# The next batch's x rounded during heads 0 and 1 and split by GpSimd in two halves, and head 0's maxima taken with 128 rows

## The reference

```python
c_adj = mean(x, channels)                              # (1024,)
Wg = adj * (symmetric function of c_adj[n] - c_adj[m]) # (1024, 1024)
g = relu(x.T @ Wg * para)                              # (256, 1024), the queries q of 4 heads of 64
k, v = split(x @ kv_w)
out[h] = softmax(q[h] @ k[h].T * scale) @ v[h]         # for 4 heads
x1 = layernorm(x + out)
```

## Time and profile before

| | us |
|---|---|
| median of 3 runs | 2891.92 |
| the profiled execution's own time | 2890.31 |
| its span, first to last instruction | 2888.4 |
| TensorE matmuls busy | 2737.2 (95%) |
| VectorE busy | 1980.6 (69%) |
| ScalarE busy | 1658.9 (57%) |
| GpSimd busy | 1276.3 (44%) |

### The profile page before, as it was taken

How to read it: one execution, slowest core, us unless ns; L and a number is a source line. 1 busy time by engine, 2 the same in 40 slices (tenths; PEclk the granted TensorE clock), 3 DMA queues, 4 the chain that set the end, 5 groups by cost and what they waited for, 6 DMA issues and landing times. The chain is left out here.

```text
span 2888.4 us, 39341 instructions
## 1 busy us (share of the span) xinstructions
PE 2737.2 (95%) x12436; PEld 1844.3 (64%) x12436; DVE 1980.6 (69%) x2843; ACT 1658.9 (57%) x2146; POOL 1276.3 (44%) x684
## 2 busy tenths in 40 slices
PE   7999999999999999999999999997699999989964
PEld 5565665656656565665656656564588888878853
DVE  6787786877868687786877868684533333348878
ACT  6566576766667666576766667663422222237768
POOL 3755657565475755657565475745200000000015
PEclk9999999999999999999999999999899999999976
DMA  4123222232222223222232222221333222305556
GB/s 139 59 83 104 76 73 75 70 105 85 68 76 80 73 83 103 76 73 74 71 104 85 69 76 80 73 66 29 119 107 104 87 87 102 109 14 197 186 228 257
DMA packets 128224, 276.23 MB, mean 96 GB/s; under 512 B 12208, under 2 KB 62384, under 8 KB 124592
## 3 DMA queue, kind: packets, MB, share of 16 engines
q1 hardware_dynamic: 128176, 275.62, 29.8%
HBM read 178.79 MB, written 62.98 MB: 84 GB/s over the span
## 5 line engine op out<-in xcount | busy, mean ns | idle before, releaser
L304 POOL TENSOR_TENSOR psum<-psum,probs 128x1024 f32<-128x1024 f32 x320 | 783.7, 2449 | 147.1 <-ACT probs L372 123.1
L372 ACT ACTIVATE probs<-sc_ps 128x1024 f32<-128x1024 f32 x512 | 507.2, 1023 | 420.4 <-PE sc_ps L813 360.0
L544 DVE TENSOR_REDUCE mx<-mx_ps 128x1 f32<-128x512 f32 x768 | 519.6, 689 | 282.3 <-PE mx_ps L782 280.5
L829 PE MATMUL pv_ps<-probs,v 128*64 128x512 f32 x2048 | 492.4, 604 | 0.0
L813 PE MATMUL sc_ps<-qa,ka 128*128 128x512 f32 x1024 | 386.9, 403 | 0.0
L813 PE MATMUL sc_ps<-qb,kb 128*128 128x512 f32 x1024 | 379.5, 393 | 0.0
L782 PE MATMUL mx_ps<-ka,qa 128*128 128x512 f32 x768 | 315.2, 424 | 11.6 <-ACT v L358 4.7
L829 PEld LDWEIGHTS pv_ps<-probs,v 128*64 128x64 f32 x2048 | 125.6, 136 | 224.8 <-issue 194.4
L782 PEld LDWEIGHTS mx_ps<-ka,qa 128*128 128x128 f32 x768 | 138.5, 187 | 184.6 <-issue 88.9
L813 PEld LDWEIGHTS sc_ps<-qa,ka 128*128 128x128 f32 x1024 | 187.6, 188 | 105.0 <-issue 64.1
L1168 DVE TENSOR_TENSOR agg_lo<-ag_ps,agg_hi 128x1024 fp32r<-128x1024 f32 x32 | 39.2, 1224 | 312.1 <-ACT agg_hi L1095 312.1
(11 more groups left out here) (194 smaller groups left out, 5551.7 us busy)
## 6 DMA issues: line engine op xcount, KB each, us to landing
adj_ring<-in_adj_dram SPq DMA_DIRECT2D x128, 512.0 KB, 3.7
pre_scratch<-pre SPq DMA_DIRECT2D x28, 1024.0 KB, 4.5
pre<-pre_scratch SPq DMA_DIRECT2D x28, 1024.0 KB, 4.9
x<-in_x_dram SPq DMA_DIRECT2D x16, 1024.0 KB, 5.6
kb<-ka SPq DMA_DIRECT2D x64, 256.0 KB, 3.3
qa<-qa SPq DMA_DIRECT2D x64, 256.0 KB, 3.1
res<-in_x_dram SPq DMA_DIRECT2D x16, 1024.0 KB, 5.7
x_scratch<-res SPq DMA_DIRECT2D x16, 1024.0 KB, 4.5
```

The lines of the kernel that those rows point to most:

```text
L304: pool.tensor_tensor(psum[:, h % 2, :], probs[:, 0, :] if k == 1 else psum[:, h % 2, :], probs[:, k % PR, :], ALU.add).then_inc(s["pool_ad ...
L372: nc.scalar.activation(probs[:, i % PR, :], sc_ps[:, t % 2, :], ACT.Exp, scale=SCALE)\
L544: nc.vector.tensor_reduce(mx2[:, nh, n:n + 1], mx_ps[:, nh, :], AX.X, ALU.max)\
L829: ins = nc.tensor.matmul(pv_ps[nh * HD:(nh + 1) * HD, h % 2, :], v[:, i, h * HD:(h + 1) * HD], probs[:, i % PR, nh * BANK:(nh + 1) * BANK] ...
```

## The change

It has four parts.

- **Head 0's maxima with 128 rows.** A new instruction on VectorE, `double_q`, writes relu of head 0's product into the other 64 rows of `qa[0]`, right from `scr`, between the two `q_times_para`. It replaces `copy_qa(b, 0)`. `max_scores` uses all 128 rows in head 0 as in the others. It now waits for `q_doubled`; ScalarE's first `relu_q`, which overwrites `scr`, waits for it too.
- **x rounded later.** The 8 tiles of `x_high` leave the stretch around `v_copy` and stand two by two behind the pairs 2 and 3 of head 0 and 0 and 1 of head 1.
- **x split in halves.** `split_x` is two instructions of 128x1024 on GpSimd, one before the additions of head 1 and one before those of head 2, each behind the last addition of the head before. TensorE's and SyncE's waits for `x_split` count two per batch.
- **Order.** In head 0 the scores' part 1 of tile 0 now stands before the first maxima of head 1 (`MAX_HALVES[0]`), and SyncE sends the row of head 0 before `copy_kb` of head 1.

```diff
-    MAX_HALVES = [[[2, 1, 1], [1, 1, 1, 1, 0], [2, 1, 1, 1, 1], [1, 1, 0, 0, 0]]] + \
+    MAX_HALVES = [[[0, 2, 1], [2, 1, 1, 1, 0], [2, 1, 1, 1, 1], [1, 1, 0, 0, 0]]] + \
...
-                copy_qa(b, 0)
                 copy_qa(b, 1)
+                store_row(b, 0)
                 copy_kb(b, 1)
-                store_row(b, 0)
...
+            def split_x(b, half):
+                tiles = slice(T // 2 * half, T // 2 * (half + 1))
+                wait(pool, s["x_split"], 2 * b + half)
+                wait(pool, s["pool_added"], POOL_ADDS * (4 * (b - 1) + half + 1))
+                wait(pool, s["xhi_done"], T * b + T // 2 * (half + 1))
+                pool.tensor_tensor(x_lo[:, tiles, :], x32[:, tiles, :], x_hi[:, tiles, :].bitcast(F32), ALU.subtract)\
                     .then_inc(s["x_split"], 1)
...
-                if not last:
-                    split_x(b + 1)
-                    wait(pool, s["x_split"], b + 2)
                 wait(pool, s["ql_done"], 4 * b + 4)
                 for h in range(HEADS):
+                    if not last and h in (1, 2):
+                        split_x(b + 1, h - 1)
+                        wait(pool, s["x_split"], 2 * b + 2 + h)
...
             def relu_q(b, c):
                 wait(act, s["qh_done"], 4 * b + 2 * c + 2)
+                if c == 0:
+                    wait(act, s["q_doubled"], b + 1)
...
-                if not last:
-                    x_high(b + 1, range(0, 4))
                 v_copy(b, 0)
-                if not last:
-                    x_high(b + 1, range(4, T))
                 v_copy(b, 1)
...
+                        if not last and 2 <= PAIRS * h + p < 2 + PAIRS:
+                            k = PAIRS * h + p - 2
+                            x_high(b + 1, range(2 * k, 2 * k + 2))
...
+            def double_q(b):
+                wait(dve, s["qt_done"], 2 * b + 1)
+                nc.vector.tensor_scalar(qa[0][other(0), :], scr[own(0), 0, :], 0.0, None, ALU.max)\
+                    .then_inc(s["q_doubled"], 1)
...
                 q_times_para(b, 0)
+                double_q(b)
                 q_times_para(b, 1)
...
                         wait(pe, s["qh_done"], 4 * b + 1)
-                        wait(pe, s["kh_done"], 4 * b + 1)
+                        wait(pe, s["q_doubled"], b + 1)
+                        wait(pe, s["kl_done"], 4 * b + 1)
...
-                    rows = slice(0, P) if h else own(h)
-                    nc.tensor.matmul(out, qa[h][rows, n * P:(n + 1) * P], ka[h][rows, nh * BANK:(nh + 1) * BANK],
+                    nc.tensor.matmul(out, qa[h][:, n * P:(n + 1) * P], ka[h][:, nh * BANK:(nh + 1) * BANK],
```

More of the change, by code:

```diff
@@ L145, in attention_layer @@
             "xth_done", "abs_done", "tanh_done", "whi_done", "kh_done", "qh_done", "v_evac", "exp_done",
-            "xhi_done", "x_split", "xtl_done", "w_done", "wlo_done", "kl_done", "qt_done",
+            "xhi_done", "x_split", "xtl_done", "w_done", "wlo_done", "kl_done", "qt_done", "q_doubled",
             "ql_done", "qr_done", "max_done", "merged", "row_done", "pool_added", "acc_done", "sum_ready", "rden_done",
@@ L163, in load_x @@
                 wait(sp, s["xt_ready"], 2 * b)
-                wait(sp, s["x_split"], b)
+                wait(sp, s["x_split"], 2 * b)
                 sp.dma_start(x32[:, :, :], x_v[b]).then_inc(s["x_in"], 16)
@@ L270, in rsqrt @@
                 pool.tensor_tensor(shift[:, :], neg_mean[:, :], rstd[:, :], ALU.mult).then_inc(s["rstd_done"], 1)
-            def split_x(b):
-                wait(pool, s["ql_done"], 4 * b)
-                wait(pool, s["xhi_done"], T * (b + 1))
-                pool.tensor_tensor(x_lo[:, :, :], x32[:, :, :], x_hi[:, :, :].bitcast(F32), ALU.subtract)\
+            def split_x(b, half):
[4 more added lines that the diff above has]
+                pool.tensor_tensor(x_lo[:, tiles, :], x32[:, tiles, :], x_hi[:, tiles, :].bitcast(F32), ALU.subtract)\
                     .then_inc(s["x_split"], 1)
@@ L305, in body @@
                                            probs[:, k % PR, :], ALU.add).then_inc(s["pool_added"], 1)
-            split_x(0)
-            pool.wait_ge(s["x_split"], 1)
+            split_x(0, 0)
+            split_x(0, 1)
+            pool.wait_ge(s["x_split"], 2)
             over_batches(pool, B, body)
@@ L737, in g_product @@
                 wait(pe, s["exp_done"], 32 * b)
-                wait(pe, s["x_split"], b + 1)
+                wait(pe, s["x_split"], 2 * b + 2)
                 for n in range(T):
@@ L800, in scores @@
                         wait(pe, s["row_done"], 4 * b + 1)
-                    if i == 0:
+                    if i == 0 and h:
                         wait(pe, qa_in[h], 16 * (b + 1))
```

## The result

| | before | after |
|---|---|---|
| median, us | 2891.89 (2890.96 to 2892.06, 4 runs) | 2871.86 (2871.24 to 2873.39, 4 runs) |
| the profiled execution's own time | 2890.31 | 2871.69 |
| its span | 2888.4 | 2869.3 |
| TensorE / VectorE busy | 2737.2 / 1980.6 | 2711.2 / 2006.3 |
| ScalarE / GpSimd busy | 1658.9 / 1276.3 | 1660.0 / 1282.6 |

The ratio is 0.9932 [0.9915, 0.9949]: faster by 20 us, 0.7%, which is small but clear of the interval. The forecast was 2870.6 us.

What follows compares the result with a forecast made beforehand. TensorE was taken to bound the first layer, losing 0.39 us per maxima cycle at edges between shapes. 16 batches gain 24.3 us, `add_last` costs 3, so 21.3 us saved: 2870.6 us, range 2859 to 2885.

Steps and rivals of the forecast that it cites:

- The tiles: Head 0's maxima on TensorE: cycle falls from 1.56 to 1.17 us, so tile 7 starts 1.6 us earlier.
- The start: Before head 0's maxima: `double_q` between VectorE's two products delays tile 2 by 0.37 us.
- If `double_q` waits for `pow`: VectorE at the start: held by GpSimd, `double_q` runs 547.85 to 548.45, second product ends near 549.6; otherwise near 548.9.
- The copy of v: After the first half of v: TensorE's wait for the copy stays exposed, and the gain there is 1.54 us.
- ScalarE has the time: it loses the rounding there: At the copy of v: ScalarE no longer rounds x there; the moved rounding counts as hidden, zero.
- The row: Head 0's row, sent by DMA before scores' part 1: TensorE waits 0 to 0.8 us, taken as 0.
- `add_last`: Edge of head 1: GpSimd's half split delays VectorE's addition, TensorE 0.2 us late in 15 batches, 3 us; head 2 0.
- The sum: Whole kernel: 24.3 us gained less 3 gives 21.3 us, so 2869.0 for the profiled execution and 2870.6 median.
- the first: Rival, chance 0.14: nothing blocks, neither `double_q` nor `add_last` is late; about 1.95 us per batch, 31 us gained, 2861.
- the second: Rival, chance 0.14: port costs in full, 0.8 us in head 1 and 0.3 in head 2; 2884, or 2880 with head 1's only.
- the third: Rival, chance 0.07: the maxima's gap comes from waits at tile edges, not 64 rows; cycle stays 1.56, 8 us slower, 2900.
- the fourth: Rival, chance 0.05: nothing measurable, waits on VectorE in head 1 give back the tiles' gain, 1.3 us more; 2890.

Runs made afterwards that it cites:

- e4: Changed kernel with only head 0's maxima matmuls back on the 64 own rows: 2901.66 us, ratio 1.0035 to the kernel before.
- e6: Changed kernel with `add_last` one tile of maxima later and TensorE's wait for ScalarE's queries placed last before head 0's first maxima: 2866.39 us.
- e1: Changed kernel with x rounded and split in its old place and the old table of head 0's maxima: 2874.48 us, ratio 0.9942.
- e3: Changed kernel with x rounded and split in its old place, the new table of maxima kept: 2875.59 us, ratio 0.9947.
- e7: e6 with one maxima half of head 0 moved from between the first two pairs to the end of the second: 2857.81 us, ratio 0.9884.
- e2: Changed kernel with only the old table of head 0's maxima restored: 2877.14 us, ratio 0.9951.
- e9: e7 with the third maxima half also moved behind tile 2 of the scores: 2857.64 us, ratio 0.9883.

## Why the prediction was right

The forecast was 2870.6 and the time 2871.86. By its own steps:

- **The tiles: right.** Five cycles of 1.17 us were said to bring tile 7 1.6 us earlier; it comes 1.66 earlier, in cycles of 1.17. That the two agree so well is partly luck: the start cost 0.17 less than said, and the five cycles won 1.86 where 2.0 were said (the sum took 5.8 us for them, 1.16 each, and the trace has 5.94). What the trace of before could only suggest, that the 0.39 us sit at the edges between shapes, e4 shows.
- **The start: 0.37 us said, 0.20 measured, for another reason.** The step that failed here is "If `double_q` waits for `pow`": it does not. The nearest row I leaned on the earlier trace rows has two operands within SBUF on VectorE; `double_q` has one, and `pow` reads 8 elements per partition in 1.7 us. Here the trace disagrees with what I took from the Trainium skill ("SBUF — State Buffer", "Who interferes with whom", the sentence on 2-port modes). It doesn't show which of the two differences lets it through; a long GpSimd instruction beside a one-source one was not tried. The product of the second half is late by 0.84 us and delays nothing: the first maxima wait for ScalarE, and VectorE's first maximum (544.66) starts 0.28 us after the product's end, released by TensorE. The 0.2 us are TensorE's steps through its list of waits (e6), and they came with the moving of x.
- **The copy of v: right at 1.54 against 1.57.** "ScalarE has the time: it loses the rounding there" is the reason that counts, and its weight was not seen: if the rounding stays, TensorE waits 0.69 us more for the copy (e1; e3 stands at the same mark).
- **The row: 0 said, 0.19 measured.** The bounds were 0 and 0.8. I took the packets' last time (563.13) for the landing, which by the semaphore's record is at 563.45 in the kernel before. Even so the row lands 0.04 us before the matmul is due; the term that I left out is the steps of TensorE's queue between the landing and the matmul. With it the gain at tile 2 is 1.36 where 1.52 was said. This is the largest error of the sum: 16 times 0.16 is 2.6 us. That three maxima then hold TensorE before tile 2 was said, and their price seen only in e7: not as a loss against before, but as 0.43 us per batch that the change leaves lying, by the two score matmuls behind the last half.
- **`add_last`: 0.2 said, 0.25 measured.** The half was to end at 584.7 and `add_last` at 585.8, 1.1 after it; it ends 1.09 after. The condition behind it, that GpSimd comes earlier because the exponentials do, held, and e2 shows what happens without it: 0.83 us. In head 2 it takes 1.68 us and no wait of TensorE follows; 0 was said.
- **The sum.** Said: 1.32 us in each of 15 batches and 1.52 in the last, 21.3 us. Measured: 1.33 in the first, 16.1 in the 14 of the loop (1.15 each), 1.78 in the last, 19.2 us. The loop's batches miss 0.17 us each: 0.16 at tile 2 and 0.05 at `add_last`, less some 0.04 that later marks win back. For the profiled execution 2869.0 us was forecast and 2871.69 measured, 2.7 more. That the median is off by 1.3 only is luck: 1.6 us were added for its distance from the profiled execution, and in the changed kernel that distance is 0.2.

Of the rivals, the first was right on `double_q` and wrong on `add_last`; the second is e2's kernel and not the changed one; the third is refuted by e4; the fourth asked for 1.3 us more on VectorE, and the change pays 0.2 for the row and 0.25 for the addition.

What stays open: e1 to e9 all keep SyncE's new order, so what the row ahead of `copy_kb` is worth alone is unmeasured; why the source's list of waits is put on the queue in another order when x is moved; and what the 0.19 us ahead of part 1 become with the wait for the row placed last.

## What to carry to other kernels

Matmuls that use fewer rows than their neighbours were not cheaper here: each change from 128 rows to 64, and each back, cost 0.2 us, and filling the unused rows with something true and useful (a copy of the queries against the keys' rest) removed 1.84 us per batch. Once a stretch is faster, look again at each engine that had room in it: the rounding of x had 1.18 us to spare before and would have cost 0.69 after, and moving it paid only together with another order of the maxima. Place a two-operand VectorE addition where GpSimd is between instructions, put the wait that is granted last at the end of a list of waits, and spread the matmuls that wait on VectorE so that no scores stand behind the last of them: these three took 14 us more without any change of the work.

## What the runs showed of the hardware

- Two 512-column matmuls of 64 rows between 256-column ones of 128 rows cost 0.39 us more than two of 128 rows (cycle 1.56 against 1.17 us, at the full clock, with nothing else changed in e4), half of it going in and half coming out. The Trainium skill ("TensorEngine Tiling (Array Packing)", "Key Properties") has the rule that a switch of mode drains the array, without a price. The starts in e4 fit that; whether 64 rows between 128 are such a switch, no run here shows.
- A wait that is already met is not free on TensorE: its queue takes one such instruction each 0.1 us (543.53, 543.63, 543.73, the load at 543.82), and with two of them ahead of the wait granted last the first matmul comes 0.18 us earlier (e6).
- A VectorE addition of 128x1024 with both operands in SBUF takes 1.22 us alone and ends 1.08 to 1.09 us after the GpSimd subtraction in which it starts, whether it started 1.36 us into it (2.13 us in all) or 0.75 (2.71). A one-source VectorE instruction ran inside GpSimd's 128x8 `pow` without being held (0.69 us), while `pow` itself took 1757 ns on average instead of 1654.
- A ScalarE copy out of PSUM of 1.02 us held TensorE for 0.65 us with nothing queued before it (changed kernel) and for 1.34 us with four roundings of 0.4 us before it (e1).
